# Block 0 of each inner layer issued alone, high parts before low parts, in a fused FFN, attention and FFN kernel

## Chip, cores and metric

One Trainium2 chip, one of its cores. The metric is the device time of one execution in microseconds (us); lower is better. The kernel before: 1492.15 us, the median of three runs (1491.34 to 1493.44).

## What is computed

A "macaron" layer over 4 sequences of 1024 rows of width 256, all float32: half a feed-forward net, attention, half the same feed-forward net again, each behind a layer norm and added to its input.

```python
def _L0_ffn_ref(x, w1_w, w1_s, ...):          # weights are -1, 0 or 1, each output has a scale
    h = silu(_tlin(x, w1_w, w1_s)) * _tlin(x, w2_w, w2_s)      # 256 -> 1024
    h = gelu(_tlin(h, h1_w, h1_s))                             # 1024 -> 1024
    h = gelu(_tlin(h, h2_w, h2_s))                             # 1024 -> 1024
    return _tlin(h, w3_w, w3_s)                                # 1024 -> 256

x = x + 0.5 * _L0_ffn_ref(_layernorm(x), ...)
x = x + _L0_attn_ref(_layernorm(x), ...)      # 16 heads, 24 fixed offsets back per row, sigmoid gate
x = x + 0.5 * _L0_ffn_ref(_layernorm(x), ...)
```

## The kernel before

**Passes.** The 4096 rows are 8 tiles of 512, and each tile goes through the net twice, so there are 16 passes of the feed-forward net. A pass is 8 input blocks (`f_in`, m = 0 to 7, two banks each, the silu half and the factor half), two inner layers of 8 hidden blocks each (`f_hidden`, layer 0 and 1, m = 0 to 7, 128 of the 1024 outputs each), and the output in two halves (`f_out`), which are issued among the next pass's input blocks, behind m = 3 and m = 7. Attention works in 16 subtiles of 256 rows (`a_...`); their steps are mixed in between the passes' steps.

**High and low parts.** To keep float32 accuracy with fp32r matmuls, every activation is held as a high part (its fp32r rounding) and a low part (the rest). In the input stage ScalarE takes the silu (`f_silu`, line 889), VectorE multiplies (`f_gate`, 984), ScalarE cuts the high part (`f_cut`, 894, mark `phi`) and GpSimd subtracts it for the low part (`f_low`, 832, mark `low`). In a hidden layer ScalarE does two gelus of one bank, one into the high part (900) and one back into the bank (901, mark `gelu`), and VectorE subtracts for the low part (`f_lo`, 975, mark `lo`). A hidden block is 16 matmuls of 512 columns: for each k of 8 one with the high part of block k of the layer before (1208) and one with its low part (1209), both with the same weights. The weights are small integers, so they have no low part; a general path for other weights exists and is not taken with these inputs (`general` is False).

**Block 0 of a layer.** It is the only one that has to wait for the activations, as they are only just being made. Its matmul pairs wait for the low part of each k (1204, 1206). In layer 1, and in both layers of pass 0, `abreast` is true and blocks 0 and 1 are issued interleaved: six k's of block 0, six k's of block 1, the last two k's of block 0, the last two of block 1 (`EARLY` = 6, lines 1217 to 1224). In layer 0 of passes 1 to 15 block 0 goes alone, high and low by turns.

**Order.** Nothing is scheduled at run time. `timeline()` and `opening()` compute a planned clock from constants (`TIMES`, `FOLLOW`, `AFTER`, `OPENING`, `STARTS`) in us: TensorE's steps follow one another with their costs, an attention step is put at the first step boundary at which it is due (`waiting`, lines 420 to 440), and what follows on other engines falls due at a fixed time behind it (`FOLLOW`, `AFTER`). Every engine, SyncE's DMA issues included, runs its own steps in the order of these due times (`schedule`), and waits on semaphores. The constants thus set places in queues, not times. The rest of a subtile hangs on the place of its first keys' projection `a_project kv0`. Among its steps: scores on VectorE (1076, 1082), exp on ScalarE (918), weighing on VectorE (1120), and GpSimd's additions (`a_add`, 815 to 828; the first group of a block of rows has none).

**Banks.** Five PSUM banks go round among `f_turn`, `f_in`, `f_hidden` and `f_out` in the planned order (lines 529 to 534); in the opening it is four. A step waits until the bank's last user has been read (`bank_free`). **Weights** of the hidden layers come through a ring of four slots (`wring`) by SyncE's DMAs (751); a slot is refilled when the block four earlier is done.

**Opening.** In pass 0 the weights still arrive: ScalarE copies each of 22 weight blocks (`w_cut`, 874), VectorE compares the copy with the original (`w_compare`, 959), and between them runs pass 0 up to the end of its layer 0 (`beginning`). Then a flag picks the path, and `timeline()` begins with layer 1 of pass 0.

Of the kernel before, what the change touches and what calls it, by code (L numbers as in the profile page):

```python
# [31 lines left out]
TIMES = [3.15, 9.24, 11.97, 4.3, 17.48, 23.96, 22.13, 3.93, 5.68, 52.96, 61.44, 3.26, 97.84, 8.0]  # L32

FOLLOW = dict(silu=-0.78, gate=0.48, cut=2.32, low=1.66, gelu=-1.23,
              lo=1.42, residual=0.59, store=2.77, fill=24.73, stats=-1.37, turn=4)


AFTER = dict(xT=-0.66, evict=0.09, keys=0.55, tanh=1.64, zT=-0.94, residual=-1.2, store=3.28, room=1.24)

OPENING = dict(block=8.36, block_step=1.78, compare=2.6, turn=7.54, half=1.61, input=10.97, count=50.87)  # L40
STARTS = [50.0, 118.2, 181.8, 275.0, 341.1, 408.3, 488.9, 564.3,
          633.8, 712.1, 780.0, 861.6, 960.9, 1034.4, 1094.4, 1168.0]
# [63 lines left out]
def macaron_kernel(nc, x, ffn_w, proj_w, out_w, cols, rows, masks, out):  # L106
# [3 lines left out]
    P = 128  # L110
# [63 lines left out]
    EARLY = 6  # L174
# [14 lines left out]
    with ctx:  # L189
# [216 lines left out]
        def abreast(r, layer):  # L406


            return layer == 1 or r.j == 0

        def timeline():
# [39 lines left out]
            for r, following in zip(passes, passes[1:] + [None]):  # L451
# [5 lines left out]
                for layer in range(0 if r.j else 1, 2):  # L457
                    for m in range(KH):
                        done = pe([6.35, 0.91, 3.63][min(m, 2)] if abreast(r, layer) else 3.63, "f_hidden", r, layer, m)
# [26 lines left out]
        def beginning(r, clock):  # L486
# [6 lines left out]
            for m in range(KH):  # L493
                steps.append((clock, "f_hidden", (r, 0, m)))
                clock += [6.35, 0.91, 3.63][min(m, 2)]
                steps += [(clock + FOLLOW[step], "f_" + step, (r, 0, m)) for step in ("gelu", "lo")]
# [39 lines left out]
        def f_bank(name, r, *rest):  # L536
            return fb[bank_of[key(name, r, *rest)]]
# [602 lines left out]
        def _(pe):  # L1140
# [45 lines left out]
            def run_hidden(r, layer, m, ring, general):  # L1186
# [4 lines left out]
                def part(to, first, stop):  # L1191
                    bank = f_bank("f_hidden", r, layer, to)

                    blocks = [to] if r is begins[0] else ring.of_step(key("f_hidden", r, layer, to))
                    if first == 0:
                        bank_free(int(general), *key("f_hidden", r, layer, to))
                        if r is begins[0]:
                            pe.wait_ge(s_hi, LOOK.index(to) + 1)
                        for i in blocks if r is not begins[0] else []:
                            pe.wait_ge(s_ring[i % 4], ring.filled(i))  # L1200
                    for k in range(first, stop):
                        if to == 0:
                            if layer == 0:
                                pe.wait_ge(r.marks.low, r.of("input", k + 1))
                            else:
                                pe.wait_ge(before.marks.lo, before.of("lo", k + 1))
                        hi = wring[:, blocks[0] % 4, k * P:(k + 1) * P]
                        pe.matmul(bank[:, :], hi, h_hi[src][:, k, :], start=(k == 0), stop=False)  # L1208
                        last = pe.matmul(bank[:, :], hi, h_lo[src][:, k, :], start=False,  # L1209
                                         stop=(not general and k == KH - 1))  # L1210
                    for k in range(KH if general and stop == KH else 0):
                        lo = wring[:, blocks[1] % 4, k * P:(k + 1) * P]
                        last = pe.matmul(bank[:, :], lo, h_hi[src][:, k, :], start=False, stop=(k == KH - 1))
                    if stop == KH:
                        last.then_inc(r.marks.mm, 1)

                if general or m > 1 or not abreast(r, layer):
# [193 lines left out]
```

## Time and profile before

| | us |
|---|---|
| median of three runs | 1492.15 |
| lowest, highest | 1491.34, 1493.44 |
| the profiled execution | 1490.28 |
| its span in the trace | 1488.5 |
| TensorE busy | 1467.6 |
| VectorE busy | 1024.2 |
| ScalarE busy | 680.6 |
| GpSimd busy | 584.7 |
| mean granted TensorE clock | 0.996 of full speed |

The profiled execution took 1490.28 us: its span of 1488.5 us and 1.8 us around it. In the rows below PE is TensorE's matmuls, PEld its weight loads, DVE is VectorE, ACT ScalarE, POOL GpSimd. A time is counted from the span's start. "L1208" is line 1208 of the kernel before. A matmul's recorded duration is longer than the distance to the next one, because they are pipelined; the distance between starts is what one costs. In square brackets stands how long the engine was idle ahead of a row and what it waited for.

### The profile page before, as it was taken

Reading aid. Unit: us, or ns where it says so; the run is one execution under the profiler, and the core shown is the slowest. Engines: PE = TensorE matmul, PEld = TensorE weight load, DVE = VectorE, ACT = ScalarE, POOL = GpSimd, SP = SyncE. Lnnn points to the kernel's source line nnn. Section 1 sums busy time; section 2 is a strip of 40 time slices with the busy share of each in tenths; the row PEclk is TensorE's granted clock in tenths of the full one; section 3 lists DMA queues with packets and bytes.
Section 4 is the critical chain, followed back from the end, with each engine's and each line's share of the span. In section 5 each row is a group of like instructions: output and inputs, shape, how many; then the busy total and the mean of one; then the engine's idle time right before and its main releaser. Section 6 shows DMA issues by size and latency. Waiting matters only on the chain.

```text
span 1488.5 us, 19211 instructions
## 1 busy us (share of the span) xinstructions
PE 1467.6 (99%) x6943; PEld 1209.9 (81%) x6943; DVE 1024.2 (69%) x1353; ACT 680.6 (46%) x1064; POOL 584.7 (39%) x530
## 2 busy tenths in 40 slices
PE   8999999999999999999999999999999999999998
PEld 6788888888878888888787888888888887878887
DVE  7534777975978777778776878685768786962322
ACT  8563544443535354444453534445353444443532
POOL 4021263552363445262644263618044527172200
PEclk9999999999999999999999999999999999999999
DMA  8855668775685875867757677584657786844232
GB/s 322 315 205 185 214 237 289 264 248 198 226 284 183 278 263 168 288 229 255 265 172 260 211 275 279 182 291 168 234 197 246 277 266 216 306 161 148 94 120 72
DMA packets 189394, 338.20 MB, mean 227 GB/s; under 512 B 15728, under 2 KB 138736, under 8 KB 188912
## 3 DMA queue, kind: packets, MB, share of 16 engines
q1 hardware_dynamic: 189296, 336.93, 66.0%
q8 instruction: 57, 0.93, 0.3%
q14 instruction: 41, 0.34, 0.1%
HBM read 314.85 MB, written 30.41 MB: 232 GB/s over the span
## 4 chain that ended last, share of the span: by engine, by line
PE 85%; DVE 5%; issue 4%; POOL 3%; ACT 2%; DMA 2%; SPq 0%; DVEq 0%; POOLq 0%; ACTq 0%
PE f_bank L1208 23%; PE f_bank L1209 23%; PE a_banks L1294 6%; PE a_banks L1208 5%; PE a_banks L1209 5%; PE f_bank L1164 5%; PE f_bank L1169 5%; PE f_bank L1239 3%; PE f_bank L1240 3%; PE a_banks L1314 2%; DVE slot L1076 1%; PE a_banks L1164 1%; PE a_banks L1169 1%; DVE S L1082 1%; POOL acc L818 1%
## 5 line engine op out<-in xcount | busy, mean ns | idle before, releaser
L1208 PE MATMUL f_bank<-h_hi,wring 128*128 128x512 f32 x1656 | 658.5, 398 | 5.4 <-POOL h_lo L832 3.4
L1209 PE MATMUL f_bank<-h_lo,wring 128*128 128x512 f32 x1656 | 647.7, 391 | 0.0
L1208 PEld LDWEIGHTS f_bank<-h_hi,wring 128*128 128x128 f32 x1656 | 312.4, 189 | 73.6 <-POOL h_lo L832 5.1
L1209 PEld LDWEIGHTS f_bank<-h_lo,wring 128*128 128x128 f32 x1656 | 312.5, 189 | 65.2 <-issue 1.4
L900 ACT ACTIVATE h_hi<-f_bank,colv 128x512 fp32r<-128x512 f32 x207 | 142.7, 689 | 438.4 <-PE f_bank L1209 438.3
L832 POOL TENSOR_TENSOR h_lo<-f_gated,h_hi 128x512 fp32r<-128x512 f32 x128 | 168.0, 1327 | 338.5 <-ACT h_hi L894 338.0
L975 DVE TENSOR_TENSOR h_lo<-f_bank,h_hi 128x512 fp32r<-128x512 f32 x207 | 141.9, 686 | 191.2 <-ACT f_bank L901 190.7
L1120 DVE TENSOR_TENSOR slot<-slot,a_banks 128x1280 f32<-128x1280 f32 (+4 forms) x124 | 169.6, 1374 | 18.2 <-DMA slot<-keys_and_values 18.2
L1076 DVE TENSOR_TENSOR slot<-slot,a_banks 128x1280 f32<-128x1280 f32 (+4 forms) x124 | 170.5, 1375 | 16.5 <-DMA slot<-keys_and_values 16.5
L1082 DVE TENSOR_REDUCE S<-slot 128x80 f32<-128x1280 f32 (+4 forms) x124 | 171.7, 1385 | 4.3
L818 POOL TENSOR_TENSOR acc<-acc,slot 128x1280 f32<-128x1280 f32 (+4 forms) x60 | 150.5, 2509 | 14.4 <-DVE slot L1120 10.7
L1208 PE MATMUL a_banks<-h_hi,wring 128*128 128x512 f32 x392 | 155.6, 397 | 0.0
L1209 PE MATMUL a_banks<-h_lo,wring 128*128 128x512 f32 x392 | 152.8, 390 | 0.0
L781 POOL TENSOR_SCALAR f_less_mean<-f_mv 128x2 f32<-128x2 f32 x32 | 7.2, 224 | 344.2 <-DVE f_mv L946 342.9
L1164 PE MATMUL f_bank<-fT_hi,w_in 128*128 128x512 f32 x416 | 133.5, 402 | 2.5 <-DVE f_gated L984 0.9
L901 ACT ACTIVATE f_bank<-f_bank,colv 128x512 f32<-128x512 f32 x207 | 135.4, 654 | 0.0
L1169 PE MATMUL f_bank<-fT_lo,w_in 128*128 128x512 f32 x416 | 128.8, 391 | 0.0
L815 POOL TENSOR_TENSOR acc<-slot 128x1280 f32<-128x1280 f32 x32 | 94.4, 2951 | 75.5 <-DVE slot L1120 75.0
L1294 PE MATMUL a_banks<-wproj,aT 128*128 128x256 f32 (+1 forms) x384 | 117.9, 450 | 0.0
L984 DVE SCALAR_TENSOR_TENSOR f_gated<-f_bank,colv,f_gated 128x512 f32<-128x512 f32 x104 | 76.4, 746 | 47.7 <-PE f_bank L1169 24.2
L894 ACT ACTIVATE h_hi<-f_gated 128x512 fp32r<-128x512 f32 x128 | 79.7, 627 | 61.7 <-DVE f_gated L984 61.6
L1239 PE MATMUL f_bank<-w_out,h_hi 128*128 128x256 f32 x408 | 98.5, 282 | 0.6 <-DVE f_gated L984 0.6
(140 smaller groups left out, 1829.6 us busy)
## 6 DMA issues: line engine op xcount, KB each, us to landing
wring<-weights_hi SPq DMA_DIRECT2D x248, 512.0 KB, 4.6
slot<-keys_and_values SPq DMA_DIRECT2D x128, 384.0 KB, 4.7
slot<-keys_and_values SPq DMA_DIRECT2D x64, 640.0 KB, 4.3
slot<-keys_and_values SPq DMA_DIRECT2D x312, 128.0 KB, 4.3
slot<-keys_and_values SPq DMA_DIRECT2D x64, 256.0 KB, 5.7
weights_hi<-in_ffn_w SPq DMA_DIRECT2D x16, 512.0 KB, 6.9
keys_and_values<-kv_out SPq DMA_DIRECT2D x32, 256.0 KB, 3.4
slot<-in_ffn_w SPq DMA_DIRECT2D x10, 512.0 KB, 6.8
```

The lines of the kernel that those rows point to most:

```text
L818: pool.tensor_tensor(acc[:, 0:count, :], acc[:, 0:count, :], slots[g][:, 0:count, :], ALU.add)\
L832: pool.tensor_tensor(h_lo[r.p][:, m, :], f_gated[:, m % 3, :], h_hi[r.p][:, m, :].bitcast(fp32), ALU.subtract).then_inc(r.marks.low, 1)
L900: act.activation(dst[:, m, :], bank[:, :], ACT.Gelu, scale=scale_col(2 + layer, m))
L1076: dve.tensor_tensor(rows_, rows_, q[:, n:n + 1, :].to_broadcast([P, count, D]), ALU.mult)\
L1082: dve.tensor_reduce(S[:, n, :, GS * g:GS * g + count].rearrange("p h e -> p e h"), rows_.rearrange("p o (h d) -> p o h d", h=HEADS), AX.X, ...
L1120: dve.tensor_tensor(rows_, rows_, weights.unsqueeze(3).to_broadcast([P, count, HEADS, DH]), ALU.mult)\
L1164: pe.matmul(bank[:, :], w12(m, w, k), fT_hi[:, k, :], start=(k == 0), stop=False)
L1169: last = pe.matmul(bank[:, :], w12(m, w, k), fT_lo[:, k, :], start=False, stop=(lo is None and k == KD - 1))
L1208: pe.matmul(bank[:, :], hi, h_hi[src][:, k, :], start=(k == 0), stop=False)
L1209: last = pe.matmul(bank[:, :], hi, h_lo[src][:, k, :], start=False, stop=(not general and k == KH - 1))
L1239: pe.matmul(to, h_hi[r.p][:, k, t], w, start=(k == 0), stop=False)
L1294: last = pe.matmul((q_bank if what == "q" else t_bank)[:, to:to + width], aT[:, k, n * P:(n + 1) * P], wproj[:, k, first:first + width], s ...
```

## The change

An inner layer's block 0 is issued alone everywhere: `abreast` and `EARLY` go. Its eight high matmuls come first, each behind a wait for the high part (mark `phi` in layer 0, `gelu` in layer 1), then its eight low matmuls, each behind a wait for the low part. All other blocks keep high and low by turns. The planned costs of blocks 0 and 1 (6.35 and 0.91) become 3.63 each, and the constants of the planned clock are set anew.

```diff
--- before.py
+++ after.py
@@ -29,17 +29,17 @@
 
 STEPS = ["stats", "turn", "kv0", "q", "kv1", "gate", "score", "score step", "ahead", "max", "weigh", "weigh step",
          "z", "out"]
-TIMES = [3.15, 9.24, 11.97, 4.3, 17.48, 23.96, 22.13, 3.93, 5.68, 52.96, 61.44, 3.26, 97.84, 8.0]
-
-FOLLOW = dict(silu=-0.78, gate=0.48, cut=2.32, low=1.66, gelu=-1.23,
-              lo=1.42, residual=0.59, store=2.77, fill=24.73, stats=-1.37, turn=4)
-
-
-AFTER = dict(xT=-0.66, evict=0.09, keys=0.55, tanh=1.64, zT=-0.94, residual=-1.2, store=3.28, room=1.24)
-
-OPENING = dict(block=8.36, block_step=1.78, compare=2.6, turn=7.54, half=1.61, input=10.97, count=50.87)
-STARTS = [50.0, 118.2, 181.8, 275.0, 341.1, 408.3, 488.9, 564.3,
-          633.8, 712.1, 780.0, 861.6, 960.9, 1034.4, 1094.4, 1168.0]
+TIMES = [3.05, 9.24, 11.97, 5.8, 17.33, 24.13, 22.13, 3.93, 5.58, 52.95, 61.44, 3.27, 97.84, 8.07]
+
+FOLLOW = dict(silu=-0.78, gate=0.48, cut=2.21, low=1.58, gelu=-0.34,
+              lo=1.29, residual=0.5, store=3.0, fill=24.73, stats=-1.33, turn=4)
+
+
+AFTER = dict(xT=-0.15, evict=0.5, keys=0.44, tanh=1.72, zT=-0.24, residual=-0.45, store=3.59, room=0.1)
+
+OPENING = dict(block=8.24, block_step=1.78, compare=2.55, turn=7.21, half=1.53, input=11.0, count=49.85)
+STARTS = [50.0, 118.2, 183.6, 275.0, 341.9, 408.3, 489.2, 565.3,
+          630.9, 712.2, 780.1, 861.7, 959.8, 1034.5, 1094.5, 1166.6]
 
 
 class Counts:
@@ -171,7 +171,6 @@
 
     OUT_AT = {3: 0, 7: 1}
     TURN_AT = FOLLOW["turn"]
-    EARLY = 6
 
     WARM = [14, 6, 9]
     LO = 2 * KH
@@ -403,11 +402,6 @@
             add_pe(at["z"] + at["out"], 1.72, "a_out", then=[("residual", "a_residual", ()), ("store", "a_store", ())])
             return steps, on_pe
 
-        def abreast(r, layer):
-
-
-            return layer == 1 or r.j == 0
-
         def timeline():
             steps, waiting, clock = [], [], 0.0
             for a in subs:
@@ -456,7 +450,7 @@
                         out_half(passes[r.j - 1], OUT_AT[m])
                 for layer in range(0 if r.j else 1, 2):
                     for m in range(KH):
-                        done = pe([6.35, 0.91, 3.63][min(m, 2)] if abreast(r, layer) else 3.63, "f_hidden", r, layer, m)
+                        done = pe(3.63, "f_hidden", r, layer, m)
                         steps += [(done + FOLLOW[step], "f_" + step, (r, layer, m)) for step in ("gelu", "lo")]
                         if following is None:
                             continue
@@ -492,7 +486,7 @@
                 steps += [(clock + FOLLOW[step], "f_" + step, (r, m)) for step in ("silu", "gate", "cut", "low")]
             for m in range(KH):
                 steps.append((clock, "f_hidden", (r, 0, m)))
-                clock += [6.35, 0.91, 3.63][min(m, 2)]
+                clock += 3.63
                 steps += [(clock + FOLLOW[step], "f_" + step, (r, 0, m)) for step in ("gelu", "lo")]
             return steps
 
@@ -1188,40 +1182,52 @@
 
                 before = begins[general] if r is FIRST else r
 
-                def part(to, first, stop):
-                    bank = f_bank("f_hidden", r, layer, to)
-
-                    blocks = [to] if r is begins[0] else ring.of_step(key("f_hidden", r, layer, to))
-                    if first == 0:
-                        bank_free(int(general), *key("f_hidden", r, layer, to))
-                        if r is begins[0]:
-                            pe.wait_ge(s_hi, LOOK.index(to) + 1)
-                        for i in blocks if r is not begins[0] else []:
-                            pe.wait_ge(s_ring[i % 4], ring.filled(i))
-                    for k in range(first, stop):
-                        if to == 0:
-                            if layer == 0:
-                                pe.wait_ge(r.marks.low, r.of("input", k + 1))
-                            else:
-                                pe.wait_ge(before.marks.lo, before.of("lo", k + 1))
-                        hi = wring[:, blocks[0] % 4, k * P:(k + 1) * P]
-                        pe.matmul(bank[:, :], hi, h_hi[src][:, k, :], start=(k == 0), stop=False)
-                        last = pe.matmul(bank[:, :], hi, h_lo[src][:, k, :], start=False,
-                                         stop=(not general and k == KH - 1))
-                    for k in range(KH if general and stop == KH else 0):
-                        lo = wring[:, blocks[1] % 4, k * P:(k + 1) * P]
-                        last = pe.matmul(bank[:, :], lo, h_hi[src][:, k, :], start=False, stop=(k == KH - 1))
-                    if stop == KH:
-                        last.then_inc(r.marks.mm, 1)
-
-                if general or m > 1 or not abreast(r, layer):
-                    part(m, 0, KH)
-                elif m == 0:
-                    part(0, 0, EARLY)
-                    part(1, 0, EARLY)
-                    part(0, EARLY, KH)
+                bank = f_bank("f_hidden", r, layer, m)
+
+                blocks = [m] if r is begins[0] else ring.of_step(key("f_hidden", r, layer, m))
+                bank_free(int(general), *key("f_hidden", r, layer, m))
+                if r is begins[0]:
+                    pe.wait_ge(s_hi, LOOK.index(m) + 1)
+                for i in blocks if r is not begins[0] else []:
+                    pe.wait_ge(s_ring[i % 4], ring.filled(i))
+
+                def high_there(k):
+
+                    if m == 0 and layer == 0:
+                        pe.wait_ge(r.marks.phi, r.of("input", k + 1))
+                    elif m == 0:
+                        pe.wait_ge(before.marks.gelu, before.of("lo", k + 1))
+
+                def low_there(k):
+                    if m == 0 and layer == 0:
+                        pe.wait_ge(r.marks.low, r.of("input", k + 1))
+                    elif m == 0:
+                        pe.wait_ge(before.marks.lo, before.of("lo", k + 1))
+
+                def high(k):
+                    return pe.matmul(bank[:, :], wring[:, blocks[0] % 4, k * P:(k + 1) * P], h_hi[src][:, k, :],
+                                     start=(k == 0), stop=False)
+
+                def low(k):
+                    return pe.matmul(bank[:, :], wring[:, blocks[0] % 4, k * P:(k + 1) * P], h_lo[src][:, k, :],
+                                     start=False, stop=(not general and k == KH - 1))
+
+                if m == 0:
+
+                    for k in range(KH):
+                        high_there(k)
+                        high(k)
+                    for k in range(KH):
+                        low_there(k)
+                        last = low(k)
                 else:
-                    part(1, EARLY, KH)
+                    for k in range(KH):
+                        high(k)
+                        last = low(k)
+                for k in range(KH if general else 0):
+                    lo = wring[:, blocks[1] % 4, k * P:(k + 1) * P]
+                    last = pe.matmul(bank[:, :], lo, h_hi[src][:, k, :], start=False, stop=(k == KH - 1))
+                last.then_inc(r.marks.mm, 1)
 
             def run_out(r, n, block, ring, general):
```

## Rows read from the trace of the kernel before

**Rows 1.** The page's head: the span, and busy time, share and instructions by engine.

```profile
span 1488.5 us, 19211 instructions
...
PE 1467.6 (99%) x6943; PEld 1209.9 (81%) x6943; DVE 1024.2 (69%) x1353; ACT 680.6 (46%) x1064; POOL 584.7 (39%) x530
```

**Rows 2.** Waits of PE, sums: line, releaser: us in total, times, longest.

```profile
PE f_bank L1208 <- POOL h_lo L832: 3.4, 1, 3.4
PE f_bank L1208 <- DVE h_lo L975: 2.1, 1, 2.1
PE a_banks L1164 <- DVE f_gated L984: 1.1, 2, 0.9
```

**Rows 3.** Groups by line: xcount, busy us, mean ns, idle before.

```profile
L1209 PE MATMUL f_bank<-h_lo,wring 128*128 128x512 f32 x1656 | 647.7, 391 | 0.0
...
L1209 PEld LDWEIGHTS f_bank<-h_lo,wring 128*128 128x128 f32 x1656 | 312.5, 189 | 65.2 <-issue 1.4
```

**Rows 4.** Timeline, PE: first matmuls of two neighbouring hidden blocks.

```profile
1457.88 0.39 PE L1208 MATMUL a_banks<-h_hi,wring 128*128 128x512 f32 x1
...
1461.50 0.39 PE L1208 MATMUL f_bank<-h_hi,wring 128*128 128x512 f32 x1
```

**Rows 5.** Timeline of the opening, 27.9 to 33 us: start, duration.

```profile
27.97 0.50 PE L1208 MATMUL f_bank<-h_hi,wring 128*128 128x512 f32 x1
...
30.04 0.62 ACT L894 ACTIVATE h_hi<-f_gated 128x512 fp32r<-128x512 f32 x1
...
31.51 0.62 ACT L894 ACTIVATE h_hi<-f_gated 128x512 fp32r<-128x512 f32 x1
...
32.21 1.30 POOL L832 TENSOR_TENSOR h_lo<-f_gated,h_hi 128x512 fp32r<-128x512 f32 x1 [0.17 <-ACT h_hi L894]
```

**Rows 6.** Timeline of the end of the opening, 57 to 60 us.

```profile
57.27 0.39 PE L1209 MATMUL f_bank<-h_lo,wring 128*128 128x512 f32 x1
...
58.97 0.69 DVE L975 TENSOR_TENSOR h_lo<-f_bank,h_hi 128x512 fp32r<-128x512 f32 x1 [3.30 <-ACT f_bank L901]
...
59.72 0.66 PE L1208 MATMUL f_bank<-h_hi,wring 128*128 128x512 f32 x1 [2.05 <-DVE h_lo L975]
```

**Rows 7.** Windows: us, busy PE, PEld, DVE, ACT, POOL, granted clock, DMA.

```profile
59.90:63.30 3.40, 3.40 (x9) 2.63 (x9) 0.00 (x0) 0.00 (x0) 0.00 (x0) 0.50 0.98 324
...
1328.10:1333.00 4.90, 3.03 (x14) 2.05 (x13) 3.08 (x3) 3.12 (x4) 4.90 (x3) 1.00 0.14 41
1333.00:1339.90 6.90, 5.38 (x12) 3.83 (x13) 2.45 (x4) 1.24 (x2) 6.76 (x5) 0.51 0.33 114
```

**Rows 8.** Timeline of pass 3, start of layer 1.

```profile
332.69 0.39 PE L1208 MATMUL a_banks<-h_hi,wring 128*128 128x512 f32 x1
...
333.48 0.65 ACT L901 ACTIVATE f_bank<-f_bank,colv 128x512 f32<-128x512 f32 x1
```

**Rows 9.** Timeline of pass 2, start of layer 1 (235.79: exp's input).

```profile
235.79 0.83 DVE L1098 TENSOR_TENSOR S<-S,mx 128x640 f32<-128x640 f32 x1
...
241.33 0.39 PE L1208 MATMUL f_bank<-h_hi,wring 128*128 128x512 f32 x1
...
242.56 0.69 ACT L900 ACTIVATE h_hi<-f_bank,colv 128x512 fp32r<-128x512 f32 x1
```

**Rows 10.** Timeline of pass 9, start of layer 1.

```profile
901.93 0.39 PE L1208 MATMUL f_bank<-h_hi,wring 128*128 128x512 f32 x1
...
905.38 0.68 DVE L975 TENSOR_TENSOR h_lo<-a_banks,h_hi 128x512 fp32r<-128x512 f32 x1
```

**Rows 11.** Timeline of pass 14, start of layer 0: POOL's queue, and PE.

```profile
1321.90 2.97 POOL L818 TENSOR_TENSOR acc<-acc,slot 128x1280 f32<-128x1280 f32 x1
...
1327.82 2.53 POOL L832 TENSOR_TENSOR h_lo<-f_gated,h_hi 128x512 fp32r<-128x512 f32 x2
...
1333.18 2.50 POOL L832 TENSOR_TENSOR h_lo<-f_gated,h_hi 128x512 fp32r<-128x512 f32 x2
...
1334.51 0.79 PE L1208 MATMUL f_bank<-h_hi,wring 128*128 128x512 f32 x1 [3.38 <-POOL h_lo L832]
```

## The prediction

> **What bounds the kernel now.** I read the page first. TensorE (PE) works 1467.6 of a span of 1488.5 us [rows 1], so only a change of PE's idle time, of its clock, or of how many matmuls it runs can move the end. The change removes and adds none. Next I read PE's waits: the long ones are 3.4 us for GpSimd's low parts, 2.1 us for VectorE's low part and 1.1 us at an input block [rows 2]; the wait at the start of the kernel lies ahead of all that is changed. Two matmuls of one hidden block start 0.227 us apart: a block of 16 took 3.62 us [rows 4]. Then I went to every place where the first block of an inner layer (m = 0) runs, 32 of them, and asked when the last high part and the last low part that it reads were written. Last came the granted clock in stretches around the two long waits [rows 7].
>
> **Part 1, the opening (pass 0, layer 0).** Before, PE runs six parts of block 0, six of block 1 and only then parts 6 and 7 of block 0, with a wait for the low part ahead of each. Block 0 began at 27.97 us; the cuts of the last two high parts end at 30.04 + 0.62 = 30.66 and 31.51 + 0.62 = 32.13, the last low part at 32.21 + 1.30 = 33.51 [rows 5]. The 24 early matmuls (5.4 us) reach to 33.4, so nothing was waited for. After, block 0 alone wants its eighth high part at 27.97 + 7 x 0.227 = 29.56. It gets it at about 32.2. Eight low matmuls and the end of the high one follow: 32.2 + 9 x 0.227 = 34.2, against 27.97 + 3.63 = 31.60. That is **+2.6 us**. Can new places bring the cut forward? From the planner's numbers, no: the eighth cut falls due at 27.77, behind the cut of weight block 10 at 26.04 and ahead of block 11 at 27.82, as before (27.85, 26.16, 27.94); the order of VectorE's products and comparisons there is the same too. What moves is the first gelu: due at 28.85 it goes ahead of w_cut 12, where ScalarE will stand until block 0 is done; block 12's comparison and load slip by 2 us, which nothing on PE asks for, since blocks 4 to 7 want cuts that come later and are paced by the gelus anyway. Can the loss be caught up? PE had no pause from then to 57.27, so I count it whole. At the end of the opening PE waits for VectorE's last low part (57.27 to 59.72 [rows 6]). I first took that for slack, but it is the bank: the 27th use of the banks falls on the bank of the 26th, and the change leaves both counts alone. The wait moves with PE.
>
> **The clock there.** After the idle 2.05 us before 59.72 the granted clock was 0.50 for 3.4 us, which costs half, 1.7 us [rows 6, 7]. The new wait is of 2.65 us, in two pieces with one matmul between. No row shows such a pair, so the price is between 0 and 1.7; nothing says which end is nearer, and I take 0.9. In a sentence of its own: the Trainium skill ("TensorE: Matmul & The Clock Gate", section "Why this matters for your kernels") warns only of idle gaps over some 3 us, by which this term would be 0; the 2.05 us of [rows 6] were enough here, so the row is taken.
>
> **Part 2, layer 1 of every pass, and the gelus' place.** Before, part 7 of block 0 was wanted 24 matmuls, 5.4 us, after the layer's start. Now the last high part is wanted after 7 (1.59 us) and the last low one after 15 (3.40 us). In the usual pass (pass 3) the layer starts at 332.69 and the two gelus of the last block end at 333.48 + 0.65 = 334.13, 1.44 us after it [rows 8]; the low part ends at 2.16. Both make it, the first by 0.15 us, which a semaphore and the held-back weight load may eat: 0 to 0.1 us in each of some ten passes, 0.5 in all. In passes 2, 6 and 10 ScalarE had an exp between the last two gelus, with a table load on each side, and the last gelu started at 242.56, 1.23 after the layer's start at 241.33 [rows 9]; in the old order each would cost 0.95 us. But gelus fall due 0.89 later than before (-0.34 for -1.23), and that puts the exp (4.53 ahead of the layer) in front of the last gelu but one (now 3.97 ahead, before 4.86). Its input was ready at 236.6, where ScalarE was idle [rows 9], so I count nothing, at worst 3 x 0.95. In pass 9 a score ahead of the last low part keeps it until 905.38 + 0.68 = 906.06, 4.13 after 901.93 [rows 10], where 3.40 is wanted: **+0.8**. Pass 13 had a like case (1.1), but the attention steps of the last subtile move there; 0, at worst 1.1.
>
> **Part 3, layer 0 of the later passes.** The high parts may now go before GpSimd's low parts are there, but the last matmul of the block still wants the last low part, as before. In 14 of 15 of these blocks PE has no wait of 0.4 us or more. The exception is **pass 14**. GpSimd added up the last subtile's values ahead of the low parts, so low parts 4 and 5 came at 1327.82 and the last two at 1333.18 to 1335.68, with one more addition between [rows 11]. PE stood 3.38 us there and was then granted half its speed for 6.8 us; 5.38 us of matmuls lie in that stretch [rows 7]: about 4.2 us idle and 2.3 of clock, 6.5 in all. High first, with the same arrivals: high parts until 3.5 us after the block's start, six low ones, and the end at 7.8 instead of 8.0 at full clock, a gain of 0.2. The idle comes in four pieces of 1.5 us or less instead of one of 3.38, so the fall of the clock may stay away: between 0 and 2.3 us, I take 1.1. The new places matter more. By hand from the planner: subtile 15 starts at 1166.6 for 1168.0, its turn falls due at 1175.84, just ahead of the step boundary at 1175.96 instead of behind it, and so its keys' projection, and all that hangs on it, goes one hidden block (3.63 us) earlier. GpSimd's queue then reads add, low 0, add, low 1 and 2, add, low 3, add, low 4 and 5, add, low 6 and 7: each addition one place forward, and one more (2.9 us) ahead of the last lows. It can start some 4.6 us sooner, since it was busy without a break from 1311 on. Net 4.6 - 2.9 = 1.7 us earlier. Bounds: 0, if VectorE's scores do not come sooner, and 3.6. Pass 14 gives back 0.2 + 1.1 + 1.7 = **3.0 us**.
>
> **Part 4, the rest.** The ring's slot of block 0 comes free after 3.63 us instead of 6.35, so its refill may start earlier; no row shows PE waiting for the ring, so 0. The other places move by steps I did not trace: the waits at input blocks, of which [rows 2] show the largest sum, are under 4 us in all, and I set 0, with 2.5 us either way. A word on weights: the pair of matmuls that the change separates reads the same 128x128 weights. The skill's same page (section "Step-by-step: what each phase is for") says that one can load weights once and multiply repeatedly, by which separating costs loads. The trace has as many loads as matmuls, 1656 and 1656 on either line, of 189 ns each beside a pitch of 227 [rows 3]; nothing was shared, so nothing is lost.
>
> **Sum.** 2.6 + 0.9 + 0.5 + 0.8 - 3.0 = +1.8 us on the profiled execution of 1490.28 us (span 1488.5). That run lies 1.87 below the median of 1492.15; on the median's footing the forecast is 1492.15 + 1.8 = 1494.0 us. A difference of 0.2%, 3 us, is about what can be told from none.
>
> **Rivals.**
> A, slower: the opening decides alone. Block 0's wait for the eighth cut (2.6) brings the clock down (1.7), and pass 14 keeps its wait because low 6 and 7 now have one more addition ahead. With part 2's 1.3 that is +5.6, 1497.8 us. For it: the opening's order is read from numbers and has no cover. Against it: GpSimd's head start. It decides as soon as pass 14 gives back less than 2.6. Chance 0.33.
> B, faster: pass 14 loses almost all of its 6.5 us, because the additions are done before the lows are due and the clock stays up, and the new places take the waits at input blocks as well (3 us), with no fall of the clock in the opening: 2.6 + 1.3 - 6 - 3 = -5.1, 1487.0 us. For it: the size of that one wait. Against it: an addition of 2.9 us still stands between the low parts. Chance 0.21.
> C, the change does nothing that counts: the freedom of high parts first is not used anywhere (in 14 of 15 layer-0 blocks nothing was waited for), and the opening's wait is caught up somewhere: 1492 to 1493 us. It shares the middle case's 0.45 with the forecast, 0.10 of it.
> D, the shared weights: if separating the pair doubled the loads of a block, 8 x 0.189 us in 32 blocks, +48 us; equal counts speak against it. Chance 0.01.
>
> **Numbers.** The forecast itself has 0.35. Faster 0.21, within 0.2% 0.45, slower 0.34 (A and D). The range 1488.5 to 1499.0 takes in A with 1 us of places on top, and on the other side the forecast less the bounds of pass 14 (2.3 - 1.1 and 3.6 - 1.7) and part of B's places.
>
> **What would show it.** Opening: a wait of PE on ScalarE's cut (line 894) of about 2.6 us between 29.5 and 32.2, and all later steps of the opening as much later; if it is absent, part 1 is wrong. Low clock just behind it or not. Passes 2, 6, 10: exp ahead of the gelu of block 6, and PE without a wait at the layer's start. Pass 9: 0.8 us on VectorE. Pass 14: GpSimd's chain beginning with an addition, PE's longest wait under 2 us. The forecast is wrong if layer 1 shows waits of over 0.3 us in most passes, or if a wait of several us turns up in a stage that had none.

## The result, and the profile after

The kernel after takes 1496.82 us (median of 7 runs, 1494.32 to 1499.53), the kernel before 1492.53 us in the same comparison (7 runs, 1491.34 to 1494.52). The ratio is 1.0032, with an interval of 1.002 to 1.0044: slower by 0.32%; the medians differ by 4.3 us. That is inside the range, but it is rival A's side: the forecast was +1.8 us, within 0.2% of before. The profiled execution took 1497.43 us, 7.1 more than the one before, since that one lay low in its spread; so I use the profiles for where the time went and the medians for how much.

The page's head of the kernel after, against [rows 1]:

```profile
span 1495.6 us, 19211 instructions
...
PE 1469.2 (98%) x6943; PEld 1208.9 (81%) x6943; DVE 1026.2 (69%) x1353; ACT 682.3 (46%) x1064; POOL 587.1 (39%) x530
```

The same instructions, and PE busy 1.6 us longer: 5.5 of the 7.1 us are idle time. PE's waits after (line, releaser: us in total, times, longest), against [rows 2]; 888 is the cut, 826 GpSimd's low part, 969 VectorE's, 1208 a high and 1212 a low matmul, 1120 the weighing:

```profile
PE f_bank L1208 <- ACT h_hi L888: 3.2, 4, 1.1
PE f_bank L1208 <- DVE h_lo L969: 2.1, 1, 2.1
PE f_bank L1212 <- POOL h_lo L826: 2.0, 2, 1.3
PE a_banks L1275 <- ACT a_hat L849: 1.4, 1, 1.4
PE a_banks L1310 <- DVE z L1120: 1.2, 2, 0.8
...
PE f_bank L1212 <- DVE h_lo L969: 0.8, 1, 0.8
```

The one long wait of before (3.4) is gone from the view. New are short ones for the cuts (two in the opening, two in pass 14), for GpSimd's and VectorE's low parts at the low matmuls, and for z; the wait for `a_hat`, the normalised rows, was 0.3 before. To place them I compared when each step of PE began in the two traces:

| stretch | after minus before, gained in it, us | forecast |
|---|---|---|
| start, ahead of all that is changed | +0.8 | 0 |
| opening, layer 0 of pass 0 | +4.2 | +2.6, clock +0.9 |
| layer 1 of pass 0 | -1.6 | 0 |
| passes 1 and 2 | +2.3 | 0, semaphores |
| passes 3 to 8 | +0.5 | semaphores (0.5 in all) |
| pass 9 | +0.8 | +0.8 |
| passes 10 to 13 | +0.7 | 0 |
| pass 14 | -0.5 | -3.0 |
| the last matmul | +7.3 | +1.8 |

Without the start these terms add up to 6.5 us, 2.2 more than the medians say: a part of them belongs to these two runs and not to the change.

**Opening.** Timeline after, PE and ScalarE from 28.7 us (start, duration; 868 is `w_cut`):

```profile
28.75 1.66 PE L1208 MATMUL f_bank<-h_hi,wring 128*128 128x512 f32 x6
31.50 0.49 PE L1208 MATMUL f_bank<-h_hi,wring 128*128 128x512 f32 x1 [1.09 <-ACT h_hi L888]
32.97 0.50 PE L1208 MATMUL f_bank<-h_hi,wring 128*128 128x512 f32 x1 [0.97 <-ACT h_hi L888]
33.31 3.19 PE L1212 MATMUL f_bank<-h_lo,wring 128*128 128x512 f32 x8
...
31.35 1.02 ACT L868 ACTIVATE a_banks<-slot 128x1024 fp32r<-128x1024 f32 x1
32.30 0.62 ACT L888 ACTIVATE h_hi<-f_gated 128x512 fp32r<-128x512 f32 x1
```

The eighth high matmul was wanted at 28.75 + 7 x 0.227 = 30.34 and began at 32.97: 2.63 us late, behind a cut that stands behind a weight block's copy. Then 3.4 us ran at half clock, which the windows show (columns as in [rows 7]):

```profile
33.80:37.20 3.40, 3.40 (x10) 2.63 (x9) 1.49 (x4) 2.13 (x4) 0.48 (x1) 0.50 0.90 323
64.70:68.10 3.40, 3.37 (x15) 2.80 (x16) 0.00 (x0) 0.00 (x0) 0.00 (x0) 1.00 1.02 377
1344.50:1347.90 3.40, 3.40 (x9) 2.66 (x9) 0.69 (x1) 0.81 (x2) 3.24 (x3) 0.50 0.47 154
```

The second row is new too: the idle 2.05 us at the end of the opening, which brought half clock in [rows 6, 7], is there again (2.06 us, up to 64.73), and the clock stayed up. So 1.6 us came back that I had not looked for.

**Pass 14.** Timeline after, GpSimd (809, 812 the additions, 826 the low parts), then PE:

```profile
1313.88 2.95 POOL L809 TENSOR_TENSOR acc<-slot 128x1280 f32<-128x1280 f32 x1 [24.11 <-DVE slot L1114]
1318.84 1.29 POOL L826 TENSOR_TENSOR h_lo<-f_gated,h_hi 128x512 fp32r<-128x512 f32 x1 [2.01 <-ACT h_hi L888]
1320.09 2.97 POOL L812 TENSOR_TENSOR acc<-acc,slot 128x1280 f32<-128x1280 f32 x1
...
1335.62 2.52 POOL L826 TENSOR_TENSOR h_lo<-f_gated,h_hi 128x512 fp32r<-128x512 f32 x2
1338.10 2.94 POOL L812 TENSOR_TENSOR acc<-acc,slot 128x1280 f32<-128x1280 f32 x1
1340.99 2.48 POOL L826 TENSOR_TENSOR h_lo<-f_gated,h_hi 128x512 fp32r<-128x512 f32 x2
...
1335.94 1.55 PE L1208 MATMUL f_bank<-h_hi,wring 128*128 128x512 f32 x6
1338.25 0.51 PE L1208 MATMUL f_bank<-h_hi,wring 128*128 128x512 f32 x1 [0.75 <-ACT h_hi L888]
1339.18 0.50 PE L1208 MATMUL f_bank<-h_hi,wring 128*128 128x512 f32 x1 [0.42 <-ACT h_hi L888]
...
1342.31 0.50 PE L1212 MATMUL f_bank<-h_lo,wring 128*128 128x512 f32 x1 [1.25 <-POOL h_lo L826]
1343.53 0.50 PE L1212 MATMUL f_bank<-h_lo,wring 128*128 128x512 f32 x1 [0.72 <-POOL h_lo L826]
```

GpSimd's order is the forecast one. But after the first addition it stands 2.01 us for low part 0, whose cut isn't there yet. The last lows end at 1343.47, 7.53 after the block's start at 1335.94; in [rows 11] they end at 1335.68, 7.52 after their block's start at 1328.16. The one wait of 3.38 us has become four, 3.14 us together, as forecast in kind; but nothing was won in the arrivals.

**Layer 1, and pass 2.** First the transposes in pass 2 whose input, `a_hat`, comes 1.4 us late; then layer 1's start in pass 2, which has no wait: on ScalarE the exp, the table load behind it and the gelu of the last block but one, then the second gelu of the last block, which nothing holds up any more, and PE; then pass 9, which has one:

```profile
196.12 0.66 PE L1275 MATMUL a_banks<-ident,a_hat 128*128 128x128 f32 x4 [1.44 <-ACT a_hat L849]
...
242.84 0.42 ACT L912 ACTIVATE a_banks<-S 128x320 f32<-128x320 f32 x1
243.28 1.28 ACT L894 ACT_TABLE_LOAD   x1
244.58 0.69 ACT L894 ACTIVATE h_hi<-f_bank,colv 128x512 fp32r<-128x512 f32 x1
...
247.75 0.65 ACT L895 ACTIVATE f_bank<-f_bank,colv 128x512 f32<-128x512 f32 x1
...
246.97 2.00 PE L1208 MATMUL f_bank<-h_hi,wring 128*128 128x512 f32 x8
248.81 2.02 PE L1212 MATMUL f_bank<-h_lo,wring 128*128 128x512 f32 x8
...
912.35 0.50 PE L1212 MATMUL f_bank<-h_lo,wring 128*128 128x512 f32 x1 [0.79 <-DVE h_lo L969]
```

### The profile page after: what moved, and what is told of

Read it like the earlier page. It is cut to its first block, busy times and chain, and to the rows that moved or that the text cites. A ratio compares the mean times of both kernels' runs of the same rounds, so it can differ in the third digit from the quotient of the medians.

```text
span 1495.6 us, 19211 instructions
## 1 busy us (share of the span) xinstructions
PE 1469.2 (98%) x6943; PEld 1208.9 (81%) x6943; DVE 1026.2 (69%) x1353; ACT 682.3 (46%) x1064; POOL 587.1 (39%) x530
## 4 chain that ended last, share of the span: by engine, by line
PE 82%; DVE 7%; POOL 4%; issue 3%; DMA 2%; ACT 2%; SPq 0%; DVEq 0%; POOLq 0%; ACTq 0%
PE f_bank L1212 23%; PE f_bank L1208 23%; PE a_banks L1212 6%; PE a_banks L1208 5%; PE a_banks L1300 5%; PE f_bank L1158 5%; PE f_bank L1163 4%; DVE slot L1070 2%; PE f_bank L1245 2%; PE f_bank L1246 2%; DMA slot<-keys_and_values 2%; DVE S L1076 2%; PE a_banks L1320 1%; POOL acc L812 1%; POOL acc L809 1%
## 5 line engine op out<-in xcount | busy, mean ns | idle before, releaser
L1208 PE MATMUL f_bank<-h_hi,wring 128*128 128x512 f32 x1656 | 629.2, 397 | 5.3 <-ACT h_hi L888 3.2
L1212 PE MATMUL f_bank<-h_lo,wring 128*128 128x512 f32 x1656 | 619.5, 392 | 2.8 <-POOL h_lo L826 2.0
L1208 PE MATMUL a_banks<-h_hi,wring 128*128 128x512 f32 x392 | 149.2, 398 | 0.0
L1212 PE MATMUL a_banks<-h_lo,wring 128*128 128x512 f32 x392 | 146.2, 390 | 0.3 <-DVE h_lo L969 0.3
L883 ACT ACTIVATE f_gated<-f_bank,colv 128x512 f32<-128x512 f32 x104 | 70.5, 686 | 63.7 <-PE f_bank L1163 52.9
```

The source lines that it names most:

```text
L1208: return pe.matmul(bank[:, :], wring[:, blocks[0] % 4, k * P:(k + 1) * P], h_hi[src][:, k, :], start=(k == 0), stop=False)
L1212: return pe.matmul(bank[:, :], wring[:, blocks[0] % 4, k * P:(k + 1) * P], h_lo[src][:, k, :], start=False, stop=(not general and k == KH ...
```

## The experiments

The theory after the result: the opening's wait decides, pass 14 gives nothing, the rest comes from the new places. The rivals: layer 1 costs more than it shows, the order "high parts first" costs or gives something by itself, the new places alone are the loss. All times are medians with the ratio to the kernel before and its interval. Runs of one kernel spread over 3 to 10 us. Differences in us are those of the medians; the ratio can differ from them by about 1 us (for e3 it gives +4.6 us and not +5.5, for e6 +10.1 and not +9.1).

**One part alone.** Block 0 goes alone and high parts first only where the condition holds; the rest of the kernel before, its constants too, stays. The two conditions, cut out of the two edits:

```diff
+if m == 0 and not general and (r is begins[0]):   # e1_opening_alone
+if m == 0 and not general and (layer == 1):       # e2_layer1_alone
+    high_first()
```

> The kernel before, with one block changed: block 0 of layer 0 in the opening goes alone, high parts first; every place in every queue and all planned costs are those of before. Theory T (the loss is the opening's wait for the eighth cut): +2.6 us from the wait and between 0 and 1.7 from the clock, so +2.6 to +4.3 on the median, a wait of PE on ScalarE's cut of about 2.6 us in the profile, and all of the loss of the changed kernel (4.3 us) or most of it. Rival R (the later layers, or the places, cost it; the opening catches its wait up): under +1 us.

Measured: 1493.88 us, 1.0005 (0.9994 to 1.0015), +1.1 us: less than theory T's +2.6 to +4.3, so the opening by itself is not most of the loss. In its trace the opening is longer by 2.6 us, with the same pair of waits, but without the fall of the clock in it, and the one behind it went as well (-1.6). 2.6 - 1.6 is 1.0, about what the median shows, but that is one run: the mean granted clock over e1's 12 runs is 0.9968, against 0.9967 over the 32 of the kernel before, so on the average of the runs the clock gave nothing back. Why the median shows only 1.1 of 2.6 stays open. Its two rows of PE's waits:

```profile
PE a_banks L1324 <- DVE z L1126: 2.9, 2, 1.6
PE f_bank L1230 <- ACT h_hi L894: 2.1, 2, 1.1
```

The first row is new and not of the opening: in passes 2 and 4 a subtile's z turn waits some 1.5 us for VectorE, in stretches whose steps no part of this edit touches. VectorE is late there because a score step in front of z waits for keys and values that a DMA brings. The same step of pass 2 in the kernel after and in e5, which is the same kernel run again:

```profile
210.15 1.49 DVE L1070 TENSOR_TENSOR slot<-slot,a_banks 128x1280 f32<-128x1280 f32 x1 [1.96 <-DMA slot<-keys_and_values]
...
210.13 1.49 DVE L1070 TENSOR_TENSOR slot<-slot,a_banks 128x1280 f32<-128x1280 f32 x1 [2.89 <-DMA slot<-keys_and_values]
```

PE's wait for z behind them is 0.83 and 1.77 us. This wait for the DMA lies between 0.45 and 2.89 us over the 14 profiles; PE waits for z in the nine where it is 1.4 us or more, each time 1.1 us less than VectorE did. So the z wait of pass 2 is a matter of the single run as much as of the kernel. What makes the DMA late isn't shown.

> The kernel before, with block 0 of layer 1 alone and high parts first in all 16 passes, all places those of before. Theory T, with its account of the exp that lies between the last two gelus in passes 2, 6 and 10 in the old order: 3 x 0.95 there, 0.8 in pass 9, 1.1 in pass 13 and under 0.5 in the rest, +4 to +5 us; with the new places the first three are gone. Rival R1 (ScalarE's last gelu is late by a little in every pass): a wait in nearly all 16 passes and over +6. Rival R2 (no matter): under +1 us.

Measured: 1497.62 us, 1.0028 (1.0016 to 1.004), +4.9 us, at the upper end of what was expected (the ratio gives +4.2). In passes 2, 6 and 10 the last gelu comes late, behind an exp and a table load. Its row of PE's waits:

```profile
PE f_bank L1230 <- ACT f_bank L901: 2.3, 3, 0.8
```

PE and ScalarE in pass 2:

```profile
246.03 0.50 PE L1230 MATMUL f_bank<-h_hi,wring 128*128 128x512 f32 x1 [0.78 <-ACT f_bank L901]
...
242.62 0.80 ACT L918 ACTIVATE a_banks<-S 128x320 f32<-128x320 f32 x2
243.44 1.28 ACT L900 ACT_TABLE_LOAD   x1
244.74 0.69 ACT L900 ACTIVATE h_hi<-f_bank,colv 128x512 fp32r<-128x512 f32 x1
```

Each of the three layers begins its fourth block 1.08 us later than before. From the exp's last instruction to the gelu's start pass 1.3 us, nearly all the table load of 1.28. The Trainium skill ("ScalarE: Activation LUTs", section "What ACT_TABLE_LOAD costs") gives about 1283 ns for the load and adds some 1380 ns of drain: the first agrees, and this trace shows no second part.

**The layer-1 repair.** e2 with those three exps placed ahead of the last gelu but one, where the new constants put them:

```diff
-            add(at["max"] + 1.8, "a_exp")
+            add(at["max"] + (1.3 if a.i in (1, 6, 11) else 1.8), "a_exp")
```

> The kernel of e2 (layer 1's block 0 alone, places of before) with three steps moved: the exp of subtiles 1, 6 and 11 goes ahead of the last gelu but one instead of between the last two. Theory T (in passes 2, 6 and 10 the wait is for the gelu behind the exp): three waits of about 1 us go, -2.5 to -3.2 us against e2, +1.7 to +2.4 against the kernel before. Rival (the late gelus as such): no difference to e2.

Measured: 1494.7 us, 1.0012 (1.0 to 1.0024), 2.4 us less than e2 by the differences to the kernel before (+2.5 against +4.9). The 1.08 us of each of the three passes are 0.04. Three moved steps of ScalarE carry it, as part 2 had reasoned.

**The places alone.** The kernel before with the new constants (the first hunk of the diff), its blocks still side by side; and the kernel after with the old constants.

> The kernel before with the new constants of the planned clock and nothing else (the blocks stay side by side). Theory T: the places alone move the time by -1 to +2 us; pass 14 keeps its wait, as in the changed kernel, and pass 2 shows the waits of about 2 us on the normalised rows that the changed kernel has. Rival P (the places carry the loss): +3 us or more. Rival Q (the places are worth something once the blocks are side by side): -2 us or less.

Measured: 1498.22 us, 1.0031 (1.0019 to 1.0043), +5.5 us: rival P's outcome, far more than theory T's -1 to +2. In its trace the loss is 2.6 us in pass 2 and 4.3 us in passes 7 and 8, at attention steps and at input blocks that wait for a bank. Of PE's waits:

```profile
PE f_bank L1208 <- POOL h_lo L832: 3.4, 1, 3.4
...
PE a_banks L1294 <- DVE kv_out L1061: 1.8, 1, 1.8
PE a_banks L1304 <- DVE z L1126: 1.6, 2, 1.2
PE a_banks L1269 <- ACT a_hat L855: 1.5, 1, 1.5
PE f_bank L1164 <- DVE xf L1043: 1.4, 1, 1.4
```

The `a_hat` wait of pass 2 is thus the new constants' own: it is 1.4 or 1.5 in all eight profiles with them, and among those with the old ones the longest of this kind is 0.6 in e6 and 0.3 in the other five. And low parts 4 and 5 still come late in pass 14.

> The changed kernel with the constants of the planned clock of before (blocks 0 alone, high parts first, planned cost 3.63 each). Theory T: the new places are worth something to blocks that go alone, since the exp goes ahead of the last two gelus in passes 2, 6 and 10: without them +1.1 (opening) + 4.9 (layer 1, as measured alone) = +6 us against the kernel before, 1.5 to 3 us slower than the changed kernel. Rival P (the new places cost 5 us whatever the blocks do, as they did alone): the old constants make it 3 to 5 us faster than the changed kernel.

Measured: 1501.21 us (5 runs), 1.0068 (1.0055 to 1.0081), +9.1 us. That is 4.5 us above the kernel after in the same comparison (e5, below): theory T's side, and more than the 1.5 to 3 us it gave. So the new constants gain 4.5 us where block 0 goes alone, and lose 5.5 where it does not. No sum of the single effects gives that; the constants fit one way of issuing. Only a part of the 4.5 us has a place in the traces: the three waits behind the exp (1.08 us each).

**The opening in the changed kernel.** First side by side again, in the kernel after (six k's of block 0, six of block 1, two and two); then the kernel as it is, again; then with the cuts brought forward.

> The changed kernel with blocks 0 and 1 of the opening's layer 0 issued side by side as before (six parts, six parts, two, two); its places and everything behind the opening as changed. Theory T: the wait at the cut goes, 2.6 to 4.3 us less than the changed kernel, so the kernel before within 1.5 us. Rival R: still +3 us or more against the kernel before.

Measured: 1491.51 us, 0.9992 (0.998 to 1.0004), 5.3 less than the kernel after and more than the 4.3 that theory T allowed the opening.

> The changed kernel itself, run again beside the others of this set: both theories expect its +4.3 us against the kernel before, within 1.5 us. The first set left a question: the opening's block alone cost +1.1 us on the kernel before, yet putting it back side by side in the changed kernel took 5 us off. If the opening costs the same in both (theory T: 1 to 3 us), this run comes out nearer +2 than +4; if +4 stands, something behind the opening takes part (rival).

Measured: 1496.66 us, 1.0031 (1.002 to 1.0042), +4.6 us: the result repeats, with both falls of the clock, in the opening and in pass 14. That is the rival's outcome: putting the opening alone costs more in the changed kernel than the 1.1 us it costs in the kernel before, so something behind the opening takes part.

The cuts brought forward; `ahead` moves all four steps of a block, in us of the planned clock:

```diff
# e7_after_cuts_early, in beginning(): silu, gate, cut and low of input blocks 5 to 7
+    ahead = {5: 0.6, 6: 1.75, 7: 2.0}.get(m, 0.0) if r is begins[0] else 0.0
-    steps += [(clock + FOLLOW[step], "f_" + step, (r, m)) for step in ("silu", "gate", "cut", "low")]
+    steps += [(clock + FOLLOW[step] - ahead, "f_" + step, (r, m)) for step in ("silu", "gate", "cut", "low")]
```

> The changed kernel with three silus, two products and two cuts of the opening's last input blocks each one weight block earlier in the queues of ScalarE and VectorE. Theory T (PE waits for the eighth cut because it stands behind a weight block's cut and comparison): the wait of 2.6 us becomes 0.3 to 1.5 us, and the opening ends 1 to 2.3 us earlier; 1 to 3 us less than the changed kernel. Rival (the wait is set by something else, the gelu or the bank): no change of the wait.

Measured: 1493.2 us, 1.0011 (1.0001 to 1.0021). Against the kernel after, as e5 stands in the same comparison, that is 3.5 us less, a little more than expected. One wait is left of the two, and the low matmuls run at full clock (x8 in 2.06 instead of 3.19 us):

```profile
29.09 2.20 PE L1209 MATMUL f_bank<-h_hi,wring 128*128 128x512 f32 x7
32.25 0.50 PE L1209 MATMUL f_bank<-h_hi,wring 128*128 128x512 f32 x1 [0.96 <-ACT h_hi L889]
32.58 2.06 PE L1213 MATMUL f_bank<-h_lo,wring 128*128 128x512 f32 x8
```

The opening grew by 1.7 us instead of 4.2: 1.0 us of the wait went (2.6 to 1.6, just outside the 0.3 to 1.5 expected), and the fall of the clock, 1.6 us. So the queue place of the cuts, behind the copies of the weights, made at least that part of the wait, which PE's new order exposed; the other 1.6 us are still there. Whether the clock stayed up because of the shorter wait isn't shown, since it also stayed up behind both waits in e1 and e6.

**High parts first, or by turns.** The kernel after with block 0 alone, but high and low in pairs:

```diff
 for k in range(KH):
-    high_there(k)
-    high(k)
-for k in range(KH):
     low_there(k)
+    high(k)
     last = low(k)
```

> The changed kernel with block 0 alone but high and low parts by turns, each pair waiting for its low part. Theory T (the last matmul of the block wants the last low part either way; the freedom of high parts first is worth 0.2 us in the opening and in pass 14, and costs nothing elsewhere): the changed kernel within 1 us. Rival (high parts first is what carries blocks that go alone): 2 us or more slower.

Measured: 1496.55 us, 1.0028 (1.0015 to 1.0041): the same as the kernel after. PE waits for GpSimd 5.2 us in 3 waits instead of 2.0 in 2, and not at all for the cuts, where the kernel after has 3.2 in 4. The freedom of the new order is worth nothing that can be measured.

**Pass 14's queue.** In the kernel before, low parts 4 to 7 go ahead of the addition that kept them:

```diff
+                    if r.j == 14 and m >= 4:
+                        steps[-1] = (1244.2 + 0.01 * m, "f_low", (r, m))
```

> The kernel before with GpSimd's low parts 4 to 7 of pass 14 ahead of the additions of the last subtile (one queue, four steps moved). Theory T (pass 14 waits for low parts queued behind additions): the wait of 3.4 us and the clock's fall there go, -4 to -6.5 us, less what the later additions cost at the last subtile's turn (0 to 4 us): between 0 and -6, likeliest -4. Rival (the additions merely move the wait to the last subtile's z and its output): within 1 us of before.

Measured: 1486.16 us (1484.43 to 1489.38), 0.997 (0.9958 to 0.9982): 5.9 us less than the kernel before, the fastest of all that ran, and faster than both. GpSimd in pass 14, then what PE's wait for the last z turn was:

```profile
1322.37 2.55 POOL L834 TENSOR_TENSOR h_lo<-f_gated,h_hi 128x512 fp32r<-128x512 f32 x2 [0.32 <-ACT h_hi L896]
1325.59 2.55 POOL L834 TENSOR_TENSOR h_lo<-f_gated,h_hi 128x512 fp32r<-128x512 f32 x2 [0.68 <-ACT h_hi L896]
1328.10 2.95 POOL L820 TENSOR_TENSOR acc<-acc,slot 128x1280 f32<-128x1280 f32 x1
...
1347.21 0.66 PE L1306 MATMUL a_banks<-ident,z 128*128 128x128 f32 x4 [0.59 <-DVE z L1128]
```

PE started the fourth block of that layer 6.5 us earlier, which is the 6.5 us that part 3 gave the wait and its clock; 0.8 goes back behind it, 0.6 of it in the last row. That is theory T's upper end, and no rival is left for this one: four steps of one queue are all that differs. The same move in the changed kernel, with the opening side by side (e9) or with the early cuts (e10), lows 3 to 7:

```diff
+                    if r.j == 14 and m >= 3:
+                        steps[-1] = (1240.7 + 0.01 * m, "f_low", (r, m))
```

> The changed kernel with the opening's blocks 0 and 1 side by side again and, in pass 14, GpSimd's low parts 3 to 7 ahead of the additions. Theory T: 1491.5 (as measured without the low parts' move) less what that move is worth, -6 on the kernel before but less here, since the additions start sooner: 1486 to 1489 us. Rival: with the new places the additions are what the last subtile waits for, and nothing is won.

> The changed kernel, its block 0 alone everywhere, with both repairs of queues: the opening's cuts one weight block earlier, and pass 14's low parts 3 to 7 ahead of the additions. Theory T: 1493.2 less 3 to 6 us, 1487 to 1490 us, so a block that goes alone costs under 2 us against one side by side when what it waits for stands right. Rival: as before.

Measured: e9 1493.58 us, 1.0009 (0.9996 to 1.0021), e10 1494.07 us, 1.001 (0.9997 to 1.0022). Both missed, and the rival came true: by the differences to the kernel before, e9 is 2.6 us slower than e4 and e10 0.7 slower than e7. In both traces PE starts the fourth block of pass 14's layer 0 5.9 us earlier than in the kernel after, and by the start of layer 1 it has lost 6.4 us again. The additions that were put back hold up the last subtile's z, and its turn stands one hidden block earlier here than in the kernel before. The row of e9:

```profile
1350.28 1.11 PE L1338 MATMUL a_banks<-ident,z 128*128 128x128 f32 x4 [3.65 <-DVE z L1122]
```

The wait moved from the low parts to z, 3.65 us of it, and brought 6.8 us of half clock with it. A later z turn in the changed kernel was not tried.

## Why the prediction was right or wrong

The measured +4.3 us lies in the range because the range is 10.5 us wide and takes in rival A; the forecast itself, +1.8, missed it by 2.5, and the account below shows that the sum's largest term is the one that failed.

**The opening's wait** was right in place, kind and size: 2.63 us for 2.6. **Its clock** was 1.6 for the 0.9 that I took, near the upper bound, in the two profiles of this kernel; e1 and e6 have the same two waits and no fall. What I missed is the other fall, at the opening's end. I had moved it along with PE as a fixed cost. It went, and the two cancel: 1.6 - 1.6 = 0 for the 0.9 that I took. The opening with its clock is worth +2.6 in the trace, for 3.5 forecast; that this comes near is luck.

**Part 2** held. Passes 2, 6 and 10 show no wait, and e2 beside e11 shows why: the exps' places are worth 2.4 us there. The semaphores cost some 0.07 us in most passes, as said; pass 9 took 0.8, for 0.8. Pass 13 was taken as 0, and its two layers took 0.6, of which 0.3 is a wait for a low part, inside the bound of 1.1.

**Pass 14** is the step that failed: -3.0 was forecast, -0.5 came. The order of GpSimd's queue was right, each addition one place forward and one more ahead of the last lows. The head start came too: the chain began at 1313.88 less the drift of 7.78, 1306.1, where before it began at 1311.05 with low part 0, 4.9 us sooner for the 4.6 forecast. The step that failed is "Net 4.6 - 2.9 = 1.7 us earlier", which lets that head start reach the last low parts. But low part 0 is second in the queue, and its cut comes with PE, when it always came. GpSimd stood idle for it, 2.01 us, and the second addition began at 1320.09 - 7.78 = 1312.31, where the first was before (1312.30). The gain is one addition (2.9 us), the loss one addition more ahead of the last lows (2.9 us): 0 for the 1.7, the lower bound I gave. I had argued from when the first item can start, and not from what stands between it and the last. Of the 0.2 for high parts first and the clock's 1.1, about 0.5 is left: in this trace the fall is 3.4 us instead of 6.8. Even that can't be credited to the change: in e1, where pass 14 is issued as before, the fall is 3.4 us as well and the pass takes 0.9 us less.

**Part 4, "the rest"**, was set to 0 and is +2.3 in passes 1 and 2, of which 1.2 is `a_hat`'s wait (1.4 for 0.3 before) and 1.0 z's, and +1.2 elsewhere. The first comes with the new constants, as e3 shows; the second is the DMA's, as told under e1, and comes with the old constants too (1.3 and 1.6 us in e1 and e2). What the constants can cost is what I had not seen: alone they cost 5.5 us. I had allowed 2.5 us either way, and had read the waits of the old places only, which show what might be won and nothing of what might be lost. Rival D is out, by equal counts of loads: 1656 and 1656 loads in the groups after, of 188 and 189 ns:

```profile
L1208 PEld LDWEIGHTS f_bank<-h_hi,wring 128*128 128x128 f32 x1656 | 311.1, 188 | 74.3 <-ACT h_hi L888 4.7
L1212 PEld LDWEIGHTS f_bank<-h_lo,wring 128*128 128x128 f32 x1656 | 312.5, 189 | 70.1 <-POOL h_lo L826 2.7
```

**Rival A** had the outcome: pass 14 kept its loss because of the addition more, and the clock fell in the opening. Its 1497.8 lies 1.0 above the median. Its name, the opening decides alone, is too strong. Rival B failed because pass 14 kept its loss, rival C because the opening's wait was not caught up. With the opening side by side the kernel equals the one before (e4), but the opening change alone costs the kernel before only 1.1 (e1). Of the 5.3 us between e4 and after, the traces show 2.6 in the opening and 1.5 in pass 14, where e4's clock stayed up; the rest is in small waits of attention steps. e6, whose opening also goes alone, has the same four waits in pass 14 and no fall there, so the opening's order doesn't bring that fall by itself; what does stays open.

## What to carry to other kernels

Where the order of every queue is written out in advance, the price of a place depends on how the other engine issues, so the constants and the issue order must be judged together: the same constants gained 4.5 us with one order and lost 5.5 with the other. To see whether a producer comes earlier, follow the queue from its head to the item that is waited for, and ask of each item between when its own input comes. And the longest wait in the profile was worth more than the change: two added lines that move four steps of one queue took 5.9 us off in the kernel before. In the kernel after, where what was moved back stood closer to its own reader, the same idea gained nothing.

## What the runs showed of the hardware

**The clock.** After PE had idled 2.05 us at the end of the opening, the granted clock was 0.50 (1.2 GHz) for 3.4 us in all seven profiles with the opening side by side (before, e2, e3, e4, e8, e9, e11), and stayed at 2.4 GHz in five of seven with the opening alone (after, e1, e5, e6, e7; not in e10 and e12), behind the same gap. What tells the two apart isn't shown. The Trainium skill ("TensorE: Matmul & The Clock Gate", section "Why this matters for your kernels") warns of idle gaps over some 3 us; here 2.05 us were enough in nine profiles of fourteen. Each such fall costs 1.6 us by the starts of PE's steps, and runs of one kernel differ in how many they have: of the kernel before in 32 runs, the three with a mean granted clock of 0.995 took 1495.7 us on average, the four with 0.998 took 1491.9. So no single profile can settle a difference of a few us.
